# A four-layer graph network on one core: scratch fills removed, masks in PSUM in all later steps, gathered rows copied to PSUM in the last layer's first step

## The reference, cut to what matters

```python
h = relu(layernorm(x)); x = x + L0(h)        # msg = h[src] * edge_weight
h = relu(layernorm(x)); x = x + L1(h)        # bilinear message, scatter
h = relu(layernorm(x)); x = x + L2(h)        # msg = (h[src] @ W_rel[type]) * e
h = relu(layernorm(x)); x = x + L3(h)
# L3: a small network makes a 16x16 matrix for every edge, once
w = gelu(gelu(edge_attr_6 @ kW1 + kb1) @ kW2 + kb2) @ kW3 + kb3
for i in range(4):                            # DEPTH = 4
    msg = einsum('ei,eio->eo', nodes[src], w)
    nodes = gelu(segment_sum(msg, dst) / deg + nodes @ root_W[i] + root_b[i])
```

## Time and profile before

| | us |
|---|---|
| median of the timed runs | 24924.08 |
| the profiled execution | 24893.96 |
| its span, first to last instruction | 24892.2 |
| PE busy (matmul) | 21275.5 |
| POOL busy | 19392.5 |
| DVE busy | 17478.9 |
| ACT busy | 14674.0 |
| fills (L781), 4,320 of them | 1422.2 |

### The profile page before, as it was taken

How to read it: one execution, slowest core, us unless ns; L and a number is a source line. 1 busy time by engine, 2 the same in 40 slices (tenths; PEclk the granted TensorE clock), 3 DMA queues, 4 the chain that set the end, 5 groups by cost and what they waited for, 6 DMA issues and landing times. The chain is left out here.

```text
span 24892.2 us, 403534 instructions
## 1 busy us (share of the span) xinstructions
PE 21275.5 (85%) x110422; PEld 11977.0 (48%) x110422; DVE 17478.9 (70%) x29340; ACT 14674.0 (59%) x24676; POOL 19392.5 (78%) x21213
## 2 busy tenths in 40 slices
PE   7999578888888999988888888799979999688886
PEld 4555255555555666654444444344434444333333
DVE  6555378888877888875555555688868888566665
ACT  7888411111115777754444444788868888577775
POOL 6777678888886888877777777777777777788887
PEclk9999789999999999998999998899989999898997
DMA  3222145555552222223333333566656666455554
GB/s 101 42 42 42 39 89 95 92 93 94 92 92 69 75 75 75 75 63 106 114 115 113 114 114 112 161 199 199 199 154 200 201 200 200 137 162 164 162 162 125
DMA packets 2192586, 2964.43 MB, mean 119 GB/s; under 512 B 778166, under 2 KB 1678244, under 8 KB 2190948
## 3 DMA queue, kind: packets, MB, share of 16 engines
q1 hardware_dynamic: 1340898, 2776.49, 34.2%
q0 software_dynamic: 782304, 157.92, 9.6%
q10 hardware_dynamic: 69282, 28.92, 0.4%
HBM read 2289.02 MB, written 672.64 MB: 119 GB/s over the span
## 5 line engine op out<-in xcount | busy, mean ns | idle before, releaser
L777 POOL DMA_INDIRECT got<-table,idx x14040 | 13721.3, 977 | 4390.6 <-issue 3967.9
L797 PE MATMUL in_place<-place_hot,tparts 128*128 128x512 fp8e4 x49950 | 11542.9, 390 | 1657.8 <-ACT place_hot L1002 1654.3
L1002 ACT ACTIVATE place_hot<-place_b,far_lanes 128x512 fp8e4<-128x512 f16 x17550 | 10959.5, 704 | 8.5 <-PE in_place L797 8.5
L797 PEld LDWEIGHTS in_place<-place_hot,tparts 128*128 128x128 bf16 x49950 | 4940.3, 101 | 7537.9 <-issue 2331.3
L1606 POOL DMA_INDIRECT added<-rows,add_idx x2160 | 3602.9, 1668 | 717.4 <-issue 659.0
L1178 DVE TENSOR_TENSOR prod<-w_in,rows_p 128x2048 f32<-128x2048 f32 x810 | 1853.1, 2288 | 1638.1 <-ACT rows_p L990 1609.8
L1649 PE MATMUL acc<-hot,spread 128*128 128x392 bf16 x12960 | 2545.2, 350 | 0.0
L1223 DVE TENSOR_TENSOR prod<-wcopy,got 128x1024 f32<-128x1024 f32 x810 | 983.6, 1231 | 1823.1 <-DMA got<-table,idx 1289.5
L1232 DVE TENSOR_REDUCE msg<-prod 128x64 f32<-128x1024 f32 x1620 | 1967.7, 1215 | 41.4
L1191 DVE TENSOR_REDUCE msg<-prod 128x128 f32<-128x2048 f32 x810 | 1853.0, 2288 | 105.4
L866 PE MATMUL wmat<-k,h 128*128 128x256 f32 x6480 | 1785.9, 400 | 0.0
(11 more groups left out here) (250 smaller groups left out, 21552.6 us busy)
## 6 DMA issues: line engine op xcount, KB each, us to landing
w_in<-kept SPq DMA_DIRECT2D x2430, 512.0 KB
kept<-wcopy SPq DMA_DIRECT2D x810, 512.0 KB, 2.7
got<-table,idx POOLq DMA_INDIRECT x14040
attr<-in_edge_attr SPq DMA_DIRECT2D x270, 768.0 KB
place_b<-place_row SPq DMA_DIRECT2D x1350, 128.0 KB
range_b<-range_row SPq DMA_DIRECT2D x1350, 128.0 KB
rows<-in_src_row SPq DMA_DIRECT2D x270, 512.0 KB
sums<-outb SPq DMA_DIRECT2D x1350, 96.0 KB
```

Of the source, the lines that this page charges most:

```text
L777: pool.indirect_dma_start(out=got[:, r, j * W:(j + 1) * W], out_offset=None, in_=table, in_offset=bass.IndirectOffsetOnAxis(ap=idx[:, r, j ...
L797: mm = pe.matmul(in_place[b][:, h, :], tparts[:, s, t, :], place_hot[:, b, t, h * XC:(h + 1) * XC], start=(t == 0 and s == 0), stop=(t == ...
L1002: ins = act.activation(place_hot[:, b, t, :], place_b[:, b, :], ACT.Abs_reciprocal_sqrt, bias=SB["far_lanes"][:, t:t + 1], scale=HOT_SLOPE ...
```

## The change

```diff
-RW = 256
-        edge_pass(nc, a, SB, "weighted", table16, fill=False)
+        edge_pass(nc, a, SB, "weighted", table16)
...
-            edge_pass(nc, a, SB, "kernel_kept" if depth else "kernel_net", table16, fill=depth == 3, psum_mask=depth >= 2)
+            edge_pass(nc, a, SB, "kernel_kept" if depth else "kernel_net", table16)
...
-        if fill:
-            rest = sb("rest", [P, J0 * RW])
...
-        if psum_mask:
+        if kind == "kernel_kept":
             mask = [ps(f"mask{k}", [P, 512])[:, 0:F * CW].rearrange(...) for k in range(HALVES)]
...
         if kind == "kernel_net":
-            h2p = [ps(f"h2p{k}", [P, GE]) for k in range(2)]
+            h2p = ps("h2p", [P, GE])
+            rows_p = ps("rows_p", [P, 512])[:, 0:J0 * W]
...   # GpSimd
-                        if kind == "kernel_kept":
+                        if kind in ("kernel_net", "kernel_kept"):
                             pool.wait_ge(S["rows_made"], k - RING + 1)
...
-                    if fill and at != 0:
-                        pool.wait_ge(S["rested"], k)
...
-                        if fill:
-                            ins = pool.memset(rest[:, j * RW:(j + 1) * RW], 0.0)
-                    if fill:
-                        ins.then_inc(S["rested"], 1)
...   # TensorE, layer2
-                    pe.wait_ge(S["h2_ready"], i * TURN_GROUPS + n + 1)
-                    pe.matmul(h2p[n % 2][:, :], SB["k2"][:, :], h1[:, n % 2, :], ...)
+                    pe.wait_ge(S["h2_ready"], i * TURN_GROUPS + n + 2)
+                    pe.matmul(h2p[:, :], SB["k2"][:, :], h1[:, n % 2, :], ...)
...   # ScalarE, kernel_net
+                    def rows_over(k, r, q, first):
+                        act.wait_ge(got_in[r], (q + 1) * (16 * J0))
+                        if not first:
+                            act.wait_ge(w_used, k * GROUPS + 2)
+                        act.activation(rows_p, got[:, r, 0:J0 * W], ACT.Copy).then_inc(S["rows_made"], 1)
...
                             copy_out(i, n, first)
+                            b, g = divmod(n, GROUPS)
+                            if g == 1:
+                                rows_over(i * HALVES + b, odd * HALVES + b, q, first and b == 0)
...   # VectorE, matrix_chunk
-                    dve.wait_ge(got_in[r], (q + 1) * (16 * J0))
+                    if kind == "kernel_net":
+                        dve.wait_ge(S["rows_made"], k + 1)
+                        rows_x = rows_p.rearrange("p (j f) -> p j f", f=W)
+                    else:
+                        dve.wait_ge(got_in[r], (q + 1) * (16 * J0))
+                        rows_x = rows_v
...
-                            bcast(rows_v[:, g * G:(g + 1) * G, 0:D], 2, D), ALU.mult).then_inc(w_used, 1)
+                            bcast(rows_x[:, g * G:(g + 1) * G, 0:D], 2, D), ALU.mult).then_inc(w_used, 1)
```

More of the change, by code:

```diff
@@ L565, in rounds, with edge_pass @@
         body(k, k % RING, k // RING, k)
-def edge_pass(nc, a, SB, kind, table, fill=True, psum_mask=False):
+def edge_pass(nc, a, SB, kind, table):
     W = 32 if kind == "relational" else 16
@@ L650, in edge_pass @@
                  "attr_used0", "attr_used1", "w_made", "w_used", "h1_made", "h1_ready", "h2_made", "h2_ready",
-                 "hot_made", "hot_used", "out_made", "stored0", "stored1", "dve_step", "run_cleared", "rested", "turn_open", "fetch_open",
+                 "hot_made", "hot_used", "out_made", "stored0", "stored1", "dve_step", "run_cleared", "turn_open", "fetch_open",
                  "place_in0", "place_in1", "range_in0", "range_in1", "places_hot", "in_place_made", "picked_made", "in_row_made", "fetched",
@@ L907, in layer2 @@
                     pe.wait_ge(S["h1_ready"], i * TURN_GROUPS + n + 3)
-                    pe.wait_ge(S["h2_ready"], i * TURN_GROUPS + n + 1)
-                    pe.matmul(h2p[n % 2][:, :], SB["k2"][:, :], h1[:, n % 2, :], start=True, stop=True).then_inc(S["h2_made"], 1)
+                    pe.wait_ge(S["h2_ready"], i * TURN_GROUPS + n + 2)
+                    pe.matmul(h2p[:, :], SB["k2"][:, :], h1[:, n % 2, :], start=True, stop=True).then_inc(S["h2_made"], 1)
                 def layer3(i, n):
@@ L940, in gelu2 @@
                         act.wait_ge(w_made, i * TURN_GROUPS + n + 1)
-                        act.activation(h2[:, n % 2, :], h2p[n % 2][:, :], ACT.Gelu_apprx_tanh, bias=SB["b2"][:, 0:1]).then_inc(S["h2_ready"], 1)
+                        act.activation(h2[:, n % 2, :], h2p[:, :], ACT.Gelu_apprx_tanh, bias=SB["b2"][:, 0:1]).then_inc(S["h2_ready"], 1)
                     def copy_out(i, n, first):
@@ L954, in copy_out, with turn @@
                         act.activation(wcopy[:, g, :], wmat[n % 2][:, :], ACT.Copy).then_inc(S["w_copied"], 1)
-                    def turn(i, first):
+                    def rows_over(k, r, q, first):
[3 more added lines that the diff above has]
+                        act.activation(rows_p, got[:, r, 0:J0 * W], ACT.Copy).then_inc(S["rows_made"], 1)
+                    def turn(i, odd, q, first):
                         last = TURN_GROUPS
@@ L966, in turn @@
                             copy_out(i, n, first)
-                    turns(act, turn)
+                            b, g = divmod(n, GROUPS)
+                            if g == 1:
+                                rows_over(i * HALVES + b, odd * HALVES + b, q, first and b == 0)
+                    turn(0, 0, 0, True)
+                    with act.Fori(0, TURNS // 2) as q:
+                        turn(q * 2 + 1, 1, q, False)
+                        turn(q * 2 + 2, 0, q + 1, False)
                     return
@@ L1247, in matrix_chunk @@
                     reduce(GROUPS - 1)
-                    dve.sem_inc(got_used[r], 1)
+                    if kind == "relational":
+                        dve.sem_inc(got_used[r], 1)
                     dve.sem_inc(attr_used[b], 1)
```

## The result

The changed kernel takes 24050.36 us in the median of four runs (24043.46 to 24060.83) against 24926.57 us for the kernel before, run beside it: a ratio of 0.9648 (0.9631 to 0.9665). That is faster, as forecast, by 876 us and not 822, and 5 us outside the range on the fast side. The two profiled executions took 24893.96 and 24043.46 us, 850.5 us apart.

What follows compares the result with a forecast made beforehand. GpSimd was taken to pace "kernel_net" and the "kernel_kept" steps, TensorE "relational"; 606 + 11 + 205 + 0 = 822 us off 24893.96 gave 24072, plus 30.1 gave 24102 us, range 24055 to 24180 (chance 0.74).

Steps and rivals of the forecast that it cites:

- lower end: Whole kernel: 24055 us, everything at its best (617 + 226 + 15 us less), with the runs 10 us lower.
- the last line of the sum: Whole kernel: 30.1 us, by which the runs' median lay above the profiled execution, added to 24072, giving 24102 us.
- Fills out of the last step: Last "kernel_kept" step: without fills it becomes the step before it, 3298 - 2692 = 606 us less.
- Masks to PSUM: Second step of layer 3: with its mask in PSUM it becomes the third, 2703 - 2692 = 11 us less.
- "relational": Pass "relational": removing fills costed at 0, range -15 to +10 us, because TensorE paces it.
- the rival: Pass "relational": GpSimd paces it after all, TensorE's modelled ends may hide waits; at most 478 us more gain, 23624; chance 0.03.
- "kernel_net": Pass "kernel_net": products reading rows from PSUM stop holding gathers up, 15.05 us a chunk; pass 4084 us, 205 less.
- The loop through `copy_out`: In "kernel_net": products, attributes, layer 1, `copy_out`, ScalarE's copy, next products; closes in 30.38 us against GpSimd's 30.10 a turn.
- long turn: In "kernel_net": a turn with layer 1 at TensorE's lower level, 30.38 us with the copy against 27.4 otherwise; most turns.
- The first rival: In "kernel_net": the copy's place eats the gain, turn stays at 31.8 us; total 24307 us; chance 0.14.
- One bank of `h2p`: In "kernel_net": layer 2 waits for the previous group's `gelu2`, 2.4 us to spare; cost 0, otherwise up to 560 us.
- Slower than before: In "kernel_net": ScalarE waiting for gathers starves TensorE, which stays at its lower level; 2481 us more, 26788; chance 0.03.

## Why the prediction was wrong

The mechanisms were right in the main and the time was not: 24050.36 against 24102 and a lower end of 24055. Of the 52 us, 23 come from the last line of the sum and 28 from its terms.

- **"The median of the runs lies 30.1 us above that execution; the same difference put on gives 24102."** This is the step that failed. The kernel before, run again, has its profiled execution 25 us above its median, and the changed kernel 7 us below its own; the difference has either sign and is no part of the kernel. I had taken three timed runs for a property of the kernel. The lower end was built on it too: 858 us at best, which does hold the 850.5 between the two profiled executions, but taken from 24924 and with only 10 us for the runs, where medians of one kernel moved by up to 55 us (24871.32 to 24926.57) between sets. The kernel before came out at 24926.57 beside the result, so the median gain there, 876, is 26 us more than the profiled one; no run says where these 26 us are, and with the changed kernel run again they are gone (848.5).
- **Fills out of the last step, 606 us**: 608.6. The step became the one before it, as read. What I left open is what the fills cost by: some 200 us of waiting, 410 of length.
- **Masks to PSUM, 11 us**: 12.4, of which 11.1 are gathers that had begun under the scan.
- **"relational", 0, with -15 to +10**: 11 between the profiles, 16 by putting the fills back. I read right that TensorE paces the pass and wrong that this makes GpSimd's fills free: they lengthen VectorE's short copies (225 to 295 ns). The 14.7 us of idle time that I named as the most to win came from a stretch that leaves out part of the pass, and was no bound: by the same marks idle time fell by 1.8 us and busy time by 9.2, so that what the rival said of modelled ends holds for these few us. Its gain near 478 us is out.
- **"kernel_net", 205 us**: 212.5. The collision of a product's two SBUF operands with a gather is shown by taking the PSUM operand away. GpSimd's pace was to be 15.05 a chunk and is 15.06. The sentence of the Trainium skill (SBUF — State Buffer, "Who interferes with whom"), by which such a product does not hold up a GpSimd-issued DMA, does not hold here: 1.162 to 1.227 us a gather against 0.946, on average over all that begin under a product.
- **The loop through `copy_out`**: its length was read right, its frequency was not. I gave a long turn 30.38 us and took 4084 for the pass. In the changed kernel's two profiles GpSimd alone sets it (4077.1 and 4072.6), and a further 0.86 us of ScalarE a chunk changes next to nothing. I had taken the turn of the earlier trace rows for the common one also after the change; before it was, in 91 of 134 turns; in the changed kernel's first profile 25 are so, and with their number the path from products to fifth `copy_out` fell from a median of 30.04 us to 28.56. Its last part (second to fifth `copy_out`, 11.57 us) did not change. Where long turns stayed common, in the profile with the fills in the last step (92 of 134), the loop paced most turns at 30.7 us and the pass took 4093.4, within the 4063 to 4101 that I had given. The first rival, a turn of 31.8 us, is out.
- **One bank of `h2p`, 0**: 0.
- **Slower than before**: nothing of it; TensorE's mean clock in the pass is 0.91, before 0.90.

The other 6 us of the 28 are in code that did not change.

## What to carry to other kernels

Where passes of one kernel differ in just the parts that a change touches, the trace of before is already the experiment: 606 of 608.6 us came from one subtraction. An instruction on an engine that paces a loop is free only as far as it fits a gap that is there anyway, and the wait that guards it can cost half as much again (some 200 beside 410 us here). Compare stretches by the same two marks: a window cut a little inside the pass made a bound of 14.7 us that was none. Forecast a ratio or a difference from one execution, and give the spread of runs, and of medians from one set of runs to the next, to the range and not to the middle.

## What the runs showed of the hardware

- A gather alone takes 0.946 us and leaves a gap of 0.305; a fill of one column (0.12 us) and the 0.19 behind it fit into that gap at no cost, 256 columns (0.33 and 0.16) lengthen the pace to 1.442 us.
- GpSimd's wait for its own last fill costs 0.70 us a chunk (189/270), though the fill it waits for lasts 0.12; with the same fills and a wait four chunks back it is gone (2715.9 us for the step).
- A gather that starts under a VectorE product with both operands in SBUF is held up to about that product's end: in the kernel before 353 of 799 are, each by what is left of the product less 0.12 to 0.13 us. Not held up are those that start in its first 0.04 us (61), in its last 0.15 us (385), or just ahead of it (0.03 us). With one operand in PSUM there is no such effect (767 gathers, 0.946 us).
- The other way round, GpSimd's fills lengthen VectorE's copies of 32 columns from 225 to 295 ns and the 90x1536 `onehot` from 620 to 700.
- Layer 1 of the fourth group takes over 1.5 us, at TensorE's lower level, in 91 of 134 turns of one kernel and in 25 to 92 of another, from one execution to the next.
